# Perceiver block on one core: K and Q stored once in float32, brought back by heads, and split there

## The chip, the cores and the metric

The kernel runs on one core of one Trainium2 chip. Its time is the device time of one execution in microseconds (us). Engines: TensorE (PE) multiplies; VectorE (DVE), ScalarE (ACT) and GpSimd (POOL) work elementwise; SyncE (SP) only issues transfers (DMAs), as GpSimd does too. The engines run in parallel, each in its own order, and wait for each other through semaphores. A transfer is carried by up to 16 DMA engines.

## The reference

A perceiver block on 256 tokens of width 2048:

```
x = x + softmax(layernorm(x) @ ctx.T) @ ctx            # ctx: 25088 x 2048
h = layernorm(x);  q, k, v = h @ Wq + bq, h @ Wk + bk, h @ Wv + bv    # (token, d, head): 64 x 32, 64 x 8, 64 x 8
k, v = repeat(k, 4 heads), repeat(v, 4 heads)
scores[s, d, e] = sum over heads h of q[s, d, h] * k[s, e, h] / 8     # within one token: 64 x 64
x = x + (softmax(scores) @ v).reshape(2048)
h = layernorm(x);  x = x + h @ W_base.T + b_base + routed experts (8 of rank 16, top 2) of h
```

The second attention is between the 64 channels of one token, summed over heads. As K is repeated over groups of 4 heads, the kernel adds up Wq in groups of 4 columns beforehand, so Q and K both are 256 tokens x 8 groups x 64 channels, and the scores of a token are one product of an 8 x 64 matrix by another.

## The kernel before, in words

**Stages.** 49 blocks of 512 context rows come first (scores, running softmax, weighted sum); they fill the span to about 2213 us and are not touched. Then the attention result is normalised, and K, Q and V are projected (n = 0, 1, 2) from the 16 chunks of the normed x. Products in float32 are made of three passes over two parts: a rounded "hi" part (ScalarE casts it) and the rest "lo" (VectorE or GpSimd subtract). The weights of each projection come in 4 pieces by SyncE (`load_w_rows`, L518), get their hi part in `next_w_piece` (L839) on ScalarE and their lo part in `lo_w_piece` (L1199) on VectorE, and signal `nat_ready[j]`. Then follows the product of the normed x with w_base, in 64 chunks of 512 output columns (`base_chunk`, L1584), w = 0 to 63: GpSimd loads a chunk of 256 KB from wt_dram to one of four buffers `tr` (`load_base`, L659; it waits for the split of the chunk four before), ScalarE makes hi (`hi_base`, L865), VectorE lo (`lo_base`, L1223; each fourth is GpSimd's), TensorE multiplies. Hi waits too for the chunk four before to be used.

**K and Q by heads.** TensorE wants, for each token m, the 8 rows of K and of Q by groups on its partitions (`k_t`, `q_t`, [P, token, 64], bfloat16), in several bfloat16 parts: `K_PARTS` and `Q_PARTS` (L1748) say which of three parts lies in which of six sets of 8 partitions, for each half of the tokens. A float32 value is the sum of three bfloat16 parts: part 0 is a cast, part 1 a cast of the rest, part 2 the rest of the rest. They are made from PSUM in the layout token by (group, channel): `first_parts` (L854, ScalarE), `rests` (L1208, VectorE), `second_parts` (L860, ScalarE), `third_parts` (L1218, VectorE). SyncE stores the three parts in `qk_dram` with `store_qk` (L556): per tile of 128 tokens 3072 runs of 128 B. `heads_back` (L562) then waits until both tiles are stored and loads them back with 12 DMAs, each of 8 partitions by 16 KB.

**Order around it.** SyncE: the V weights, store of K (L569), the rows of lora_a (L572, in runs of 128 B), return of K (L574), store of Q (L575), return of Q (L578), b_base (L580). ScalarE (L883 to L898): first and second parts of K between the weight pieces, hi of w = 0 to 3, the V weight pieces, first and second parts of Q, copy of V, then hi of w = 4 and up (L915), with the groups of A, the gate and V's transposed groups (`v_group`, L900) put in after fixed chunks: those of `A_AFTER`, `GATE_AFTER`, `V_AFTER` (L1752 to L1756), each behind the hi of the chunk four further on. VectorE (L1238 to L1253) has the same order. TensorE: projection (L1564), `base_chunk` 0 to 15 with those groups (L1619); after w = 14 it waits for the returns of K and Q (L1643) and makes the scores of the first 8 of 128 pairs of tokens (`pair_scores`, L1597). After w = 15 each step has scores, transposes and three chunks.

Of the kernel before, what the change touches and what calls it, by code (L numbers as in the profile page):

```python
# [5 lines left out]
F32 = mybir.dt.float32  # L6
U32 = mybir.dt.uint32
ALU = mybir.AluOpType
# [4 lines left out]
BF16 = mybir.dt.bfloat16  # L13

P = 128
# [13 lines left out]
def perceiver_block(nc, x, ctx, wq, bq, wk, bk, wv, bv, w_base, b_base, w_gate, lora_a, lora_b, out):  # L29
# [11 lines left out]
    _, TOK, DIM = x.shape  # L41
    KEYS = ctx.shape[1]
    DH, HEADS = bq.shape
    KVH = bk.shape[1]
    REP = HEADS // KVH
    EXPERTS, RANK, _ = lora_a.shape
    OUTF = w_base.shape[0]
    TT = TOK // P
# [3 lines left out]
    NB = KEYS // KB  # L52
    PIECES = 4
    QKC = DH * KVH
# [57 lines left out]
    with ExitStack() as stack:  # L112
        def sem(name):
            return stack.enter_context(nc.semaphore(name))
# [10 lines left out]
        def put(at, name, shape, dt=F32):  # L125
            return nc.alloc_sbuf_tensor_at(name, shape, dt, offset=at)
# [7 lines left out]
        KIB = 1024  # L134
# [5 lines left out]
        at_probs = room(22 * KIB)  # L140
# [37 lines left out]
        w_rows = (put(at_quart + 24 * KIB, "w_rows0", [P, KT, BANK]), put(at_probs + 12 * KIB, "w_rows1", [P, KT, BANK]),  # L178
                  put(at_raw, "w_rows2", [P, KT, BANK]), put(at_raw + 8 * KIB, "w_rows3", [P, KT, BANK]))
        a_nat = put(at_quart + 24 * KIB, "a_nat", [P, DIM])  # L180
        k_nat = put(at_probs, "k_nat", [P, TT, 3, QKC], BF16)
        q_nat = put(at_quart, "q_nat", [P, TT, 3, QKC], BF16)
        qk_rest = put(at_quart + 6 * KIB, "qk_rest", [P, TT, QKC])
        a_sum = put(at_quart + 10 * KIB, "a_sum", [P, QKC])
# [80 lines left out]
        warm = late("warm", [P, 4])  # L265

        ps = stack.enter_context(nc.psum_tensor("ps", [P, 8, BANK], F32))
        qk_dram = nc.dram_tensor("qk_dram", (2, 3, KVH, TOK, DH), BF16)
        wq_dram = nc.dram_tensor("wq_dram", (DIM, QKC), F32)
        wt_dram = nc.dram_tensor("wt_dram", (DC, P, OUTF), F32)  # L270
        wp_dram = nc.dram_tensor("wp_dram", (PC, P, OUTF), F32)
# [18 lines left out]
        nat_ready = [sem(f"nat_ready{j}") for j in range(PIECES)]  # L290
# [25 lines left out]
        pool_split = sem("pool_split")  # L316
        w_used = sem("w_used")
        qkv_done = sem("qkv_done")
        qk_part1 = sem("qk_part1")
        qk_rested = sem("qk_rested")  # L320
        qk_part2 = sem("qk_part2")
# [98 lines left out]
        def _(sp):  # L420
# [14 lines left out]
            def load_in_chunks(to, src, a, done):  # L435

                sp.dma_start(to.rearrange("p (c a i) -> p a c i", a=QR, i=SQ)[:, a],
                             src[:, a * QF:(a + 1) * QF].rearrange("p (c i) -> p c i", i=SQ)).then_inc(done, 16)
# [112 lines left out]
            for n, rows in ((1, wq_rows), (2, wv_rows)):  # L551
                for j in range(PIECES):
                    sp.wait_ge(nat_ready[j], NB + n)
                    load_w_rows(j, rows)

            def store_qk(n, w, of):  # L556
                for t in range(TT):
                    sp.wait_ge(qk_split, TT * n + t + 1)
                    sp.dma_start(qk_dram[w, :, :, t * P:(t + 1) * P].rearrange("s g m d -> m (s g) d"),  # L559
                                 of[:, t].rearrange("p s (g d) -> p (s g) d", d=DH)).then_inc(qk_stored, 16)  # L560

            def heads_back(w, to, parts):  # L562
                sp.wait_ge(qk_stored, TT * (2 - w) * 16)
                for k, part in enumerate(parts):
                    for t in range(TT):
                        at = P // TT * t + KVH * k
                        sp.dma_start(to[at:at + KVH], qk_dram[w, part, :, t * P:(t + 1) * P]).then_inc(qk_back, 16)

            store_qk(0, 1, k_nat)  # L569
            sp.wait_ge(nat_ready[0], NB + 3)  # L570
            for a in range(QR):
                load_in_chunks(a_nat[:], lora_a.rearrange("e r d -> (e r) d"), a, a_loaded)  # L572
            sp.wait_ge(nat_ready[1], NB + 3)
            heads_back(1, k_t, K_PARTS)  # L574
            store_qk(1, 0, q_nat)  # L575
            for j in range(2, PIECES):
                sp.wait_ge(nat_ready[j], NB + 3)
# [155 lines left out]
        def _(act):  # L733
# [105 lines left out]
            def next_w_piece(n, j):  # L839
                if j < PIECES - 1:  # L840
                    w_piece(n, j, w_used, (PIECES - 1) * (n - 1) + j + 1)
                else:
                    w_piece(n, j, qkv_done, TT * n)
# [7 lines left out]
            deviation(1, 1)  # L851
            hi_x_tile(G_X1, 1)

            def first_parts(n, to):  # L854
                for t in range(TT):
                    act.wait_ge(qkv_done, n * TT + t + 1)
                    act.copy(to[:, t, 0].rearrange("p (g d) -> p g d", g=KVH),
                             ps[:, QKV_BANKS[n] + t, :].rearrange("p (d g) -> p g d", g=KVH)).then_inc(qk_part1, 1)

            def second_parts(n, to):  # L860
                for t in range(TT):
                    act.wait_ge(qk_rested, n * TT + t + 1)
                    act.copy(to[:, t, 1], qk_rest[:, t]).then_inc(qk_part2, 1)
# [18 lines left out]

            for j in range(PIECES - 1):  # L883
                next_w_piece(1, j)
            first_parts(0, k_nat)
            next_w_piece(1, PIECES - 1)
            second_parts(0, k_nat)
            for w in range(RING_CH):
                hi_base(w)
            for j in range(PIECES - 1):  # L890
                next_w_piece(2, j)
            next_w_piece(2, PIECES - 1)
            first_parts(1, q_nat)
            second_parts(1, q_nat)
            act.wait_ge(qkv_done, 3 * TT)
            src = ps[:, QKV_BANKS[2], :].rearrange("p (d g) -> p g d", g=KVH)
# [96 lines left out]
        def _(dve):  # L993
# [205 lines left out]
            def lo_w_piece(n, j):  # L1199
                dve.wait_ge(nat_hi_ready, (NB + n) * PIECES + j + 1)  # L1200
                dve.tensor_tensor(nat_lo[:, j], w_rows[j][:], nat_hi[:, j].bitcast(F32), ALU.subtract).then_inc(nat_ready[j], 1)  # L1201
# [3 lines left out]
            normalise(1, acc, x_nat)  # L1205
            lo_x_tile(G_X1, 1)

            def rests(n, of):  # L1208
                for t in range(TT):
                    dve.wait_ge(qk_part1, TT * n + t + 1)  # L1210
                    if n > 0:
                        dve.wait_ge(qk_split, TT * (n - 1) + t + 1)
                    dve.tensor_tensor(qk_rest[:, t].rearrange("p (g d) -> p g d", g=KVH),
                                      ps[:, QKV_BANKS[n] + t, :].rearrange("p (d g) -> p g d", g=KVH),
                                      of[:, t, 0].rearrange("p (g d) -> p g d", g=KVH),
                                      ALU.subtract).then_inc(qk_rested, 1)

            def third_parts(n, of):  # L1218
                for t in range(TT):
                    dve.wait_ge(qk_part2, TT * n + t + 1)  # L1220
                    dve.tensor_tensor(of[:, t, 2], qk_rest[:, t], of[:, t, 1], ALU.subtract).then_inc(qk_split, 1)
# [13 lines left out]
                dve.tensor_scalar(base_x[:, 1, ob * KB:(ob + 1) * KB], ps[:, 1, :], ln_b[:, 1:2], None,  # L1235
                                  ALU.mult).then_inc(base_kept[1], 1)

            for j in range(PIECES - 1):  # L1238
                lo_w_piece(1, j)
            rests(0, k_nat)  # L1240
            lo_w_piece(1, PIECES - 1)
            third_parts(0, k_nat)
            for w in range(RING_CH):
                if not by_pool(w):
                    lo_base(w)
            for j in range(PIECES):
                lo_w_piece(2, j)
            rests(1, q_nat)
            third_parts(1, q_nat)
            dve.wait_ge(qkv_done, 3 * TT)  # L1250
            src = ps[:, QKV_BANKS[2] + 1, :].rearrange("p (d g) -> p g d", g=KVH)
# [179 lines left out]
        def _(pe):  # L1431
# [132 lines left out]
            for n in (1, 2):  # L1564
                if n == 1:
                    pe.wait_ge(acc_updated, 8 * NB + 2)
                if n == 2:
                    pe.wait_ge(qk_rested, TT)
                for t in range(TT):
                    projection_bias(n, t)  # L1570
                for c in range(DC):
                    if c % 4 == 0:
                        pe.wait_ge(nat_ready[c // 4], NB + n + 1)
                    for t in range(TT):
                        projection(n, c, t)
# [43 lines left out]
            for w in range(PRE_W):  # L1619
                base_chunk(w)  # L1620
                if w in A_AFTER:
                    if 0 in A_AFTER[w]:
                        pe.wait_ge(a_loaded, 16 * QR)
                        pe.wait_ge(qk_rested, 2 * TT)
                    for g in A_AFTER[w]:
                        group(G_A + g, MID_BANK + (G_A + g) % 2, [chunk_cols(a_nat, 4 * g + a) for a in range(4)])
                if w == GATE_AFTER:
                    pe.wait_ge(gate_loaded, 16 * QR)
                    gate_group(G_GATE, side_rows, DC)
                if w == SUM_AFTER:  # L1630
                    pe.wait_ge(a_summed, 2 * (2 + PC))
                    group(G_SUM, MID_BANK + G_SUM % 2, [chunk_cols(a_sum, a) for a in range(PC)])
                if w == GSUM_AFTER:
                    gate_group(G_GSUM, gate_sum, PC)
                if w in V_AFTER:
                    if 0 in V_AFTER[w]:
                        for t in range(TT):
                            pe.wait_ge(v_copied[t], 2)
                    for k in V_AFTER[w]:
                        t, half = k // 2, k % 2  # L1640
                        plain_group(H_V + k, [v_dup[:, t, 4 * half + a].rearrange("p r e -> p (r e)") for a in range(4)])
                if w == PRE_W - 2:
                    pe.wait_ge(qk_back, 16 * TT * (len(Q_PARTS) + len(K_PARTS)))  # L1643
                    pe.wait_ge(lo_drained, G_GSUM + 1)
                    pair_scores(0)
# [136 lines left out]
```

## Time and profile before

| | us |
|---|---|
| median of 3 runs | 2508.55 (2503.86 to 2513.61) |
| profiled execution, its own time | 2506.24 |
| its span, first to last instruction | 2504.5 |
| TensorE busy | 2453.2 (98%) |
| VectorE, GpSimd, ScalarE busy | 1948.7, 1420.5, 1093.8 |
| mean granted clock of TensorE | 0.994 |

Busy time is time in which an instruction runs. The chain of waits follows the work back from the last instruction, at each step to what released it. Times in rows count from the start of the span. In a timeline row, the bracket at the end is the idle time of that engine just before and what ended it.

### The profile page before, as it was taken

To read this page: it belongs to the slowest core of one execution; us is meant where nothing else is said; L and a number is where in the kernel's file an instruction comes from. 1 tells how busy PE (TensorE), PEld (TensorE's weight loads), DVE (VectorE), ACT (ScalarE), POOL (GpSimd) and SP (SyncE) were. 2 spreads that over 40 slices of the span, in tenths; PEclk is the share of its full clock that TensorE was granted. 3 is DMA by queue.
4 is the path that set the end of the run, shared out by engine and by line. 5 is a ranking of instruction groups with operands and counts; after the bars stand their busy time and mean duration, and the time that the engine had idled before them with its cause. 6 is when DMAs were issued, how large, how long until landed. Compare 5 with 4: busy or idle time off the path is not lost.

```text
span 2504.5 us, 36094 instructions
## 1 busy us (share of the span) xinstructions
PE 2453.2 (98%) x11446; PEld 2009.8 (80%) x11446; DVE 1948.7 (78%) x2702; ACT 1093.8 (44%) x1576; POOL 1420.5 (57%) x1056
## 2 busy tenths in 40 slices
PE   6999999999999999999999999999999999999899
PEld 4788888888888888888888888888888888877677
DVE  7878888888888888888788887888878878674356
ACT  4444444444444444444444444444444444333443
POOL 4466666666666555565566565565555655652441
PEclk9999999999999999999999999999999999999899
DMA  9887878888788988889888988888888898778633
GB/s 239 212 229 203 229 210 220 224 206 229 206 229 217 224 206 219 222 211 218 212 219 204 230 212 204 219 217 219 211 219 216 205 222 217 199 169 155 153 122 101
DMA packets 421112, 518.22 MB, mean 207 GB/s; under 512 B 54407, under 2 KB 296071, under 8 KB 418441
## 3 DMA queue, kind: packets, MB, share of 16 engines
q1 hardware_dynamic: 411080, 475.66, 77.9%
q0 software_dynamic: 9984, 41.95, 5.0%
q8 instruction: 28, 0.46, 0.1%
q14 instruction: 20, 0.16, 0.0%
HBM read 488.71 MB, written 28.84 MB: 207 GB/s over the span
## 4 chain that ended last, share of the span: by engine, by line
PE 92%; DVE 3%; DMA 2%; SPq 1%; ACT 1%; issue 0%; POOL 0%; ACTq 0%; POOLq 0%
PE ps L1435 30%; PE ps L1437 30%; PE ps L1436 29%; PE ps L1444 2%; DMA tr<-wt_dram 2%; DVE ch_lo L1061 1%; SPq L429 1%; DMA raw<-in_ctx_dram 1%; SPq L559 0%; DVE tr L1057 0%; PE ps L1656 0%; DVE nat_lo L1201 0%; PE ps L1729 0%; PE ps L1602 0%; PE ps L1463 0%
## 5 line engine op out<-in xcount | busy, mean ns | idle before, releaser
L608 POOL TENSOR_TENSOR nat_lo<-raw,nat_hi 128x512 fp32r<-128x512 f32 x784 | 1170.9, 1523 | 874.0 <-ACT nat_hi L767 841.2
L1061 DVE TENSOR_TENSOR ch_lo<-tr,ch_hi 128x512 fp32r<-128x512 f32 x784 | 849.0, 1083 | 369.2 <-ACT ch_hi L756 369.2
L756 ACT CAST ch_hi<-tr 128x512 fp32r<-128x512 f32 x784 | 477.2, 621 | 807.6 <-PE ps L1437 799.4
L1435 PE MATMUL ps<-ch_hi,xt_hi 128*128 128x512 f32 x1696 | 680.1, 401 | 19.0 <-DVE ch_lo L1061 7.9
L1437 PE MATMUL ps<-ch_hi,xt_lo 128*128 128x512 f32 x1696 | 665.0, 392 | 0.0
L1436 PE MATMUL ps<-ch_lo,xt_hi 128*128 128x512 f32 x1696 | 664.1, 392 | 0.0
L1435 PE MATMUL ps<-nat_hi,pt_hi 128*128 128x512 f32 x1568 | 611.7, 390 | 2.1 <-DVE pt_lo L1010 2.1
L1437 PE MATMUL ps<-nat_hi,pt_lo 128*128 128x512 f32 x1568 | 610.3, 389 | 0.0
L1436 PE MATMUL ps<-nat_lo,pt_hi 128*128 128x512 f32 x1568 | 610.1, 389 | 0.0
L1057 DVE STREAM_TRANSPOSE tr<-quart 128x512 f32<-128x512 f32 x784 | 547.1, 698 | 0.0
L767 ACT CAST nat_hi<-raw 128x2048 fp32r<-128x2048 f32 x196 | 374.5, 1911 | 207.3 <-PE ps L1437 194.5
L1435 PEld LDWEIGHTS ps<-ch_hi,xt_hi 128*128 128x128 f32 x1696 | 320.4, 189 | 88.2 <-DVE ch_lo L1061 9.5
L1437 PEld LDWEIGHTS ps<-ch_hi,xt_lo 128*128 128x128 f32 x1696 | 320.1, 189 | 69.0
L1436 PEld LDWEIGHTS ps<-ch_lo,xt_hi 128*128 128x128 f32 x1696 | 321.0, 189 | 62.0
L1435 PEld LDWEIGHTS ps<-nat_hi,pt_hi 128*128 128x128 f32 x1568 | 294.3, 188 | 67.1 <-issue 3.4
L1437 PEld LDWEIGHTS ps<-nat_hi,pt_lo 128*128 128x128 f32 x1568 | 294.3, 188 | 61.4
L1436 PEld LDWEIGHTS ps<-nat_lo,pt_hi 128*128 128x128 f32 x1568 | 294.3, 188 | 60.8
L1099 DVE SCALAR_TENSOR_TENSOR acc<-acc,alpha,ps 128x512 f32<-128x512 f32 x248 | 177.8, 717 | 26.5 <-PE ps L1437 25.6
L740 ACT CAST pt_hi<-ps 128x512 fp32r<-128x512 f32 x98 | 57.2, 584 | 120.8 <-PE ps L1444 120.8
L1108 DVE SCALAR_TENSOR_TENSOR acc<-acc,alpha,ps 128x512 f32<-128x512 f32 x144 | 101.2, 703 | 4.9 <-PE ps L1437 4.9
L1226 DVE TENSOR_TENSOR ch_lo<-tr,ch_hi 128x512 fp32r<-128x512 f32 x56 | 40.9, 737 | 77.3 <-ACT ch_hi L872 76.9
L773 ACT ACTIVATE probs<-ps,neg_max 128x512 f32<-128x512 f32 x98 | 67.1, 685 | 77.4 <-DVE neg_max L1081 77.4
(199 smaller groups left out, 1312.7 us busy)
## 6 DMA issues: line engine op xcount, KB each, us to landing
quart<-in_ctx_dram SPq DMA_DIRECT2D x392, 512.0 KB, 8.3
raw<-in_ctx_dram SPq DMA_DIRECT2D x196, 1024.0 KB, 8.3
wq_in<-in_L_attn_Wq_dram POOLq DMA_DIRECT2D x16, 1024.0 KB, 6.3
win<-in_L_ffn_W_base_dram SPq DMA_DIRECT2D x64, 256.0 KB, 6.8
tr<-wt_dram POOLq DMA_DIRECT2D x64, 256.0 KB, 3.2
wt_dram<-stage SPq DMA_DIRECT2D x32, 256.0 KB, 5.6
wt_dram<-stage_b SPq DMA_DIRECT2D x32, 256.0 KB, 10.3
wq_dram<-wq_out POOLq DMA_DIRECT2D x16, 256.0 KB, 2.3
```

The source lines that it names most:

```text
L608: last = pool.tensor_tensor(nat_lo[:, j, t], raw[:, j % 2, t], nat_hi[:, j, t].bitcast(F32), ALU.subtract)
L740: act.copy(dst, src).then_inc(hi_drained, 1)
L756: act.copy(ch_hi[:, c % RING_CH, :], tr[:, c % RING_TR, :]).then_inc(chunk_hi, 1)
L767: act.copy(nat_hi[:, j], raw[:, j % 2]).then_inc(nat_hi_ready, 1)
L773: act.activation(probs[:, q, :], ps[:, SCORE_BANK + TT * new + q, :], ACT.Exp, bias=neg_max[:, new, q:q + 1], accum_out=row_sum[:, q:q + 1 ...
L1057: dve.transpose(tr[:, c % RING_TR, :].rearrange("p (r i) -> p r i", i=SQ), src).then_inc(chunk_transposed, 1)
L1061: dve.tensor_tensor(ch_lo[:, c % RING_CH, :], tr[:, c % RING_TR, :], ch_hi[:, c % RING_CH, :].bitcast(F32), ALU.subtract).then_inc(chunk_s ...
L1099: dve.scalar_tensor_tensor(piece, piece, alpha[:, 1 - turn.parity, q:q + 1], ps[:, out_bank(v, turn.over), :], ALU.mult, ALU.add).then_inc ...
L1108: dve.scalar_tensor_tensor(piece, piece, alpha[:, turn.parity, q:q + 1], ps[:, out_bank(v, False), :], ALU.mult, ALU.add).then_inc(acc_upd ...
L1435: pe.matmul(out_, a_hi, b_hi, start=start, stop=False)
L1436: pe.matmul(out_, a_hi, b_lo, start=False, stop=False)
L1437: return pe.matmul(out_, a_lo, b_hi, start=False, stop=stop)
```

## The change

K and Q are copied from PSUM once, in float32, to `k_full` and `q_full` (ScalarE, `full_copy`), stored to a new `full_dram` in runs of 256 B (`store_full`), and come back with each partition holding 8 tokens of one group, a run of 2 KB (`full_by_heads`). The three parts are made there, as before but from SBUF, and `store_qk` stores them in runs of 1 KB. `heads_back` loads the same bytes in the same DMAs of 8 partitions by 16 KB, from a `qk_dram` in which each tile's part is contiguous. The orders: SyncE stores and brings back K before it loads lora_a, stores K's parts behind that, then stores Q, returns K by heads, brings Q's rows back, stores Q's parts. ScalarE and VectorE make K's parts between the second and third V weight piece, and Q's before V's copy, where they were. TensorE waits for `qk_copied` where it waited for `qk_rested`.

```diff
-        k_nat = put(at_probs, "k_nat", [P, TT, 3, QKC], BF16)
+        k_full = put(at_probs, "k_full", [P, TT, QKC])
+        k_nat = put(at_probs + 4 * KIB, "k_nat", [P, TT, 3, QKC], BF16)
+        q_full = put(at_probs + 16 * KIB, "q_full", [P, TT, QKC])
...
-        qk_dram = nc.dram_tensor("qk_dram", (2, 3, KVH, TOK, DH), BF16)
+        qk_dram = nc.dram_tensor("qk_dram", (2, 3, TT, KVH, P, DH), BF16)
+        full_dram = nc.dram_tensor("full_dram", (2, TT, KVH, P, DH), F32)
...
+            def store_full(n, of):
+                for t in range(TT):
+                    sp.wait_ge(qk_copied, TT * n + t + 1)
+                    sp.dma_start(full_dram[n, t].rearrange("g m d -> m g d"),
+                                 of[:, t].rearrange("p (g d) -> p g d", d=DH)).then_inc(full_stored[n][t], 16)
+
+            def full_by_heads(n, to):
+                for t in range(TT):
+                    sp.wait_ge(full_stored[n][t], 16)
+                    sp.dma_start(to[:, t], full_dram[n, t].rearrange("g (a b) d -> (g a) (b d)", a=P // KVH)
+                                 ).then_inc(full_back[n][t], 16)
+
             def store_qk(n, w, of):
                 for t in range(TT):
                     sp.wait_ge(qk_split, TT * n + t + 1)
-                    sp.dma_start(qk_dram[w, :, :, t * P:(t + 1) * P].rearrange("s g m d -> m (s g) d"),
-                                 of[:, t].rearrange("p s (g d) -> p (s g) d", d=DH)).then_inc(qk_stored, 16)
+                    sp.dma_start(qk_dram[w, :, t].rearrange("s g (a b) d -> (g a) s (b d)", a=P // KVH),
+                                 of[:, t]).then_inc(qk_stored, 16)
...
-                        sp.dma_start(to[at:at + KVH], qk_dram[w, part, :, t * P:(t + 1) * P]).then_inc(qk_back, 16)
-
-            store_qk(0, 1, k_nat)
+                        sp.dma_start(to[at:at + KVH], qk_dram[w, part, t]).then_inc(qk_back, 16)
+
+            store_full(0, k_full)
+            full_by_heads(0, k_full)
             sp.wait_ge(nat_ready[0], NB + 3)
             for a in range(QR):
                 load_in_chunks(a_nat[:], lora_a.rearrange("e r d -> (e r) d"), a, a_loaded)
+            store_qk(0, 1, k_nat)
+            store_full(1, q_full)
             sp.wait_ge(nat_ready[1], NB + 3)
             heads_back(1, k_t, K_PARTS)
+            full_by_heads(1, q_full)
             store_qk(1, 0, q_nat)
...
-            def first_parts(n, to):
+            def full_copy(n, to):
                 for t in range(TT):
                     act.wait_ge(qkv_done, n * TT + t + 1)
-                    act.copy(to[:, t, 0].rearrange("p (g d) -> p g d", g=KVH),
-                             ps[:, QKV_BANKS[n] + t, :].rearrange("p (d g) -> p g d", g=KVH)).then_inc(qk_part1, 1)
+                    act.copy(to[:, t].rearrange("p (g d) -> p g d", g=KVH),
+                             ps[:, QKV_BANKS[n] + t, :].rearrange("p (d g) -> p g d", g=KVH)).then_inc(qk_copied, 1)
+
+            def first_parts(n, of, to):
+                for t in range(TT):
+                    act.wait_ge(full_back[n][t], 16)
+                    act.copy(to[:, t, 0], of[:, t]).then_inc(qk_part1, 1)
...
-            first_parts(0, k_nat)
+            full_copy(0, k_full)
             next_w_piece(1, PIECES - 1)
-            second_parts(0, k_nat)
             for w in range(RING_CH):
                 hi_base(w)
-            for j in range(PIECES - 1):
+            for j in range(2):
                 next_w_piece(2, j)
+            first_parts(0, k_full, k_nat)
+            second_parts(0, k_nat)
+            next_w_piece(2, 2)
+            act.wait_ge(nat_ready[1], NB + 3)
+            full_copy(1, q_full)
             next_w_piece(2, PIECES - 1)
-            first_parts(1, q_nat)
+            first_parts(1, q_full, q_nat)
             second_parts(1, q_nat)
...
-                    dve.tensor_tensor(qk_rest[:, t].rearrange("p (g d) -> p g d", g=KVH),
...
+                    dve.tensor_tensor(qk_rest[:, t], full[:, t], of[:, t, 0], ALU.subtract).then_inc(qk_rested, 1)
...
-            for j in range(PIECES - 1):
+            for j in range(PIECES):
                 lo_w_piece(1, j)
-            rests(0, k_nat)
-            lo_w_piece(1, PIECES - 1)
-            third_parts(0, k_nat)
             for w in range(RING_CH):
                 if not by_pool(w):
                     lo_base(w)
-            for j in range(PIECES):
+            for j in range(2):
                 lo_w_piece(2, j)
-            rests(1, q_nat)
+            rests(0, k_full, k_nat)
+            third_parts(0, k_nat)
+            for j in range(2, PIECES):
+                lo_w_piece(2, j)
+            rests(1, q_full, q_nat)
             third_parts(1, q_nat)
...
                 if n == 2:
-                    pe.wait_ge(qk_rested, TT)
+                    pe.wait_ge(qk_copied, TT)
...
-                        pe.wait_ge(qk_rested, 2 * TT)
+                        pe.wait_ge(qk_copied, 2 * TT)
```

## Rows read from the trace of the kernel before

**Rows 1.** The chain that ended last, share of the span by engine.

```profile
PE 92%; DVE 3%; DMA 2%; SPq 1%; ACT 1%; issue 0%; POOL 0%; ACTq 0%; POOLq 0%
```

**Rows 2.** Stretches: us; PE, PEld, DVE, ACT, POOL busy (x); PEclk, DMA share, GB/s.

```profile
2282.00:2306.00 24.00, 24.00 (x102) 18.83 (x102) 6.08 (x5) 4.08 (x5) 8.07 (x11) 1.00 0.80 113
...
2312.00:2332.00 20.00, 18.67 (x106) 14.71 (x106) 8.24 (x15) 9.99 (x19) 7.97 (x12) 1.00 0.91 179
...
2340.00:2356.00 16.00, 12.43 (x56) 8.82 (x57) 6.29 (x10) 8.74 (x13) 7.16 (x10) 0.52 0.50 163
```

**Rows 3.** Timeline of TensorE: start, us, operation, idle before and its end.

```profile
2340.34 0.79 PE L1435 MATMUL ps<-ch_hi,xt_hi 128*128 128x512 f32 x1 [7.27 <-DVE ch_lo L1226]
...
2345.39 0.87 PE L1602 MATMUL ps<-k_t,q_t 48*64 48x64 bf16 x16 [2.13 <-DMA q_t<-qk_dram]
```

**Rows 4.** Timeline of SyncE's issues, 2263 to 2325 us.

```profile
2263.87 10.39 SPq L559 DMA_DIRECT2D qk_dram<-k_nat  x2
2274.31 8.01 SPq L437 DMA_DIRECT2D a_nat<-in_L_ffn_A_dram  x4
2282.43 6.12 SPq L567 DMA_DIRECT2D k_t<-qk_dram  x12
2288.93 25.34 SPq L559 DMA_DIRECT2D qk_dram<-q_nat  x2
2319.64 4.47 SPq L567 DMA_DIRECT2D q_t<-qk_dram  x12
```

**Rows 5.** DMA view of 2272.5:2278, 2278.5:2285.5, 2286:2290 and 2326:2330, in this order.

```profile
DMA packets 6199, 0.85 MB, mean 155 GB/s; under 512 B 6173, under 2 KB 6173, under 8 KB 6198
...
DMA packets 7676, 0.98 MB, mean 141 GB/s; under 512 B 7675, under 2 KB 7675, under 8 KB 7675
...
q1 hardware_dynamic: 82, 0.27, 51.7%
...
q1 hardware_dynamic: 68, 0.56, 96.4%
```

**Rows 6.** Landing: K store; Q store; tiles issued 2290:2296; tiles issued after 2354.

```profile
DMA to landing us min/median/max: 12.5/13.7/14.9
...
DMA to landing us min/median/max: 27.2/28.2/29.1
...
DMA to landing us min/median/max: 17.3/18.2/19.2
...
DMA to landing us min/median/max: 2.8/2.9/4.9
```

**Rows 7.** Timeline of ScalarE: hi of w = 4, 13, V's copies, w = 14, 15, 16.

```profile
2310.66 1.16 ACT L872 CAST ch_hi<-tr 128x512 fp32r<-128x512 f32 x2 [3.43 <-DMA tr<-wt_dram]
...
2326.51 0.62 ACT L872 CAST ch_hi<-tr 128x512 fp32r<-128x512 f32 x1 [2.08 <-DMA tr<-wt_dram]
2327.04 2.57 ACT L907 COPY v_t<-ps 64x256 f32<-64x256 f32 x4
2338.94 0.62 ACT L872 CAST ch_hi<-tr 128x512 fp32r<-128x512 f32 x1 [9.34 <-DMA tr<-wt_dram]
2342.61 0.62 ACT L872 CAST ch_hi<-tr 128x512 fp32r<-128x512 f32 x1 [3.05 <-DMA tr<-wt_dram]
...
2345.85 0.62 ACT L872 CAST ch_hi<-tr 128x512 fp32r<-128x512 f32 x1
```

**Rows 8.** Timeline of GpSimd: loads of w = 13, 14 and 16 issued.

```profile
2319.09 0.54 POOL L671 DMA_DIRECT2D tr<-wt_dram  x1 [0.20 <-issue]
2321.78 0.54 POOL L671 DMA_DIRECT2D tr<-wt_dram  x1 [2.15 <-DVE ch_lo L1226]
...
2325.46 0.54 POOL L671 DMA_DIRECT2D tr<-wt_dram  x1 [0.74 <-DVE ch_lo L1226]
```

**Rows 9.** K's first and third parts: duration ns min/median/max, starts, shapes.

```profile
L857 ACT CAST k_nat<-ps x2: 572/578/585, 2255.9 to 2256.8; 128x512 bf16<-128x512 f32 x2
...
L1221 DVE TENSOR_TENSOR k_nat<-qk_rest,k_nat x2: 684/686/687, 2261.7 to 2262.3; 128x512 bf16<-128x512 f32 x2
```

More of the change, by code:

```diff
@@ L318, in perceiver_block @@
         qkv_done = sem("qkv_done")
+        qk_copied = sem("qk_copied")
+        full_stored = [[sem(f"full_stored{n}_{t}") for t in range(TT)] for n in range(2)]
+        full_back = [[sem(f"full_back{n}_{t}") for t in range(TT)] for n in range(2)]
         qk_part1 = sem("qk_part1")
@@ L1206, in _, with rests @@
             lo_x_tile(G_X1, 1)
-            def rests(n, of):
+            def rests(n, full, of):
                 for t in range(TT):
@@ L1212, in rests @@
                         dve.wait_ge(qk_split, TT * (n - 1) + t + 1)
-                    dve.tensor_tensor(qk_rest[:, t].rearrange("p (g d) -> p g d", g=KVH),
-                                      ps[:, QKV_BANKS[n] + t, :].rearrange("p (d g) -> p g d", g=KVH),
-                                      of[:, t, 0].rearrange("p (g d) -> p g d", g=KVH),
-                                      ALU.subtract).then_inc(qk_rested, 1)
+                    dve.tensor_tensor(qk_rest[:, t], full[:, t], of[:, t, 0], ALU.subtract).then_inc(qk_rested, 1)
             def third_parts(n, of):
```

## The prediction

> **What bounds the kernel now.** I read the chain of waits first: TensorE holds 92% of it [rows 1], and the 49 blocks of context, some 2200 us, are full. The change touches none of that. It touches the stretch from 2255 to 2355 us, where K, Q and V are projected and the first 16 chunks of w_base (I call them w = 0 to 15, and their 256 KB loads from wt_dram "tiles") are multiplied. So the second view is busy time by stretch [rows 2]: TensorE is full until 2312, then has 18.67 of the 20 us to 2332 and 12.43 of the 16 from 2340, these at a granted clock of 0.52, about its lower level of 1.2 GHz. The TensorE timeline [rows 3] names the holes: 7.27 us before w = 14, which waited for its low part and behind it for its tile (ScalarE sat 9.34 us on the transfer, [rows 7]), and 2.13 us for q_t.
>
> Behind both stands one thing, read from SyncE's row [rows 4] beside the DMA view [rows 5]. The return of K by heads (12 DMAs, each 8 partitions by 16 KB) is issued at 2282.43, the one of Q at 2319.64. While the K return runs alone (2286 to 2290) the hardware queue moves 0.27 MB and fills only 51.7% of the 16 engines: half the engines carry it, at 67 GB/s. All 12, 1.57 MB, take 23.4 us at that rate. The store of Q is issued at 2288.93 behind it and lands 27 to 29 us later [rows 6], although SyncE's second half of that issue was merely stuck on the queue. Q's own return then takes from 2319.64 to the first scores at 2345.39, 25.75 us. Tiles that are loaded beside such a return land after 17.3 to 19.2 us, and after 2.8 to 4.9 once it is over [rows 6].
>
> **The change, part by part.** Call S the time at which the return of Q is first issued; now S = 2319.64.
>
> *K out.* The K copies read PSUM as the first parts did (0.58 us each, [rows 9]) and cost nothing new. The store is now 2048 pieces of 256 B instead of 6144 of 128 B. The latter ran from about 2272.5, when the V weights were through, to 2278: 0.85 MB in 5.5 us, 155 GB/s [rows 5]. Half a megabyte takes 1.8 us if the cost goes by pieces (2048 of 6199 in 5.5 us) and 3.4 us if it goes by bytes; I take 2.5 and 1.2 for landing, so 2276.2. It landed at 2279.2 (2264.3 plus 14.9).
>
> *K back in rows.* New: two loads of 256 KB, 128 rows of 2 KB each. Nearest row: a tile of the same size and row length, 2.8 to 4.9 us; with a busy queue 17. I take 3, so 2279.2. SyncE waits there, and behind it stand only the lora_a loads: they were issued from 2274.31 over 8.01 us, and start now at 2276.5.
>
> *K's parts.* Two casts, two subtractions, two casts, two subtractions, staggered over the two tiles, 0.58 and 0.69 us each: four links and one extra, 2.7 us, so 2281.9. This wait is new on ScalarE and VectorE. Behind it on ScalarE is the third V weight piece, which starts at 2281 rather than 2276.9 and whose low part is done at 2285.2. TensorE is full from 2282 to 2306 with V's 16 chunks [rows 2], 1.4 us each from 2284, and wants this piece at the ninth, 2295. Cover 10 us: cost nothing. If the K rows came after 2289 it would cost TensorE one for one.
>
> *K's store.* 0.79 MB in pieces of 1 KB, issued behind lora_a. lora_a's small pieces drained until 2285.5 [rows 5], and shift to about 2286. At 200 GB/s the store needs 3.7 us and lands at 2290.9, between 2289 and 2293 (by 155 GB/s). The Q copy's store (0.5 MB) is ahead of the return in the queue and fits into that landing. The K return moves from 2282.43, with data from 2285.5, to data from 2292: about 7 us later, ended at 2316.3 and not 2309.5.
>
> *Q back in rows.* In SyncE's order `full_by_heads(1, ...)` comes after `heads_back(1, ...)`. Its rows use all engines, hence also the half that is busy until 2316.3. So it lands at 2319.8 at best: 0.5 MB is 2.4 us, 1.1 for landing. From below: were it not held it would land near 2300; from above, if it fares as a tile beside a return, 2323.
>
> *Q's parts and store.* 3.0 us for the chain, until 2322.8; the store, 0.79 MB, lands 5.2 us later (its second half took as much after SyncE came free at 2314.3). S = 2328.0, 8.4 us later than now. What is removed, the 25.34 us in which SyncE was held at L559, buys nothing: nobody but this same return stood behind it, and the K return ahead of it stays.
>
> *Who waits behind Q's parts.* On both engines the copies of V and then all splits of w = 4 and up stand behind them. Now hi of w = 4 ran at 2310.66 [rows 7]; it will be 2323.1, after two V copies of 0.6 us each. TensorE has w = 0 to 3, ends them at 2312.3 and then idles until A's third group at 2326.3: 14 us. By itself this is hidden, since TensorE now waits at w = 14 until 2340.3 anyhow. But the tiles fall behind: there are four buffers, and the load of w + 4 is issued after the split of w. Now the load of w = 13 is issued 0.55 us before S, w = 14 at S + 2.1, w = 16 at S + 5.8 [rows 8], and they are cast at S + 6.9, S + 19.3 and S + 26.2, w = 15 at S + 23.0 [rows 7]: a tile issued after S comes near the end of the Q return. In the new order the loads of w = 11, 12 and 13 are issued at about S + 1.4, S + 3.3 and S + 5.8. So tile 13 is cast between S + 23.0 (as w = 15 now) and S + 26.2 (as w = 16). And two of V's transposed groups, which TensorE needs after w = 11, are copied by ScalarE behind the cast of w = 13: 2.57 us more [rows 7]. TensorE then does w = 12, 13, 14 and the first scores; q_t is there by then.
>
> **The sum.** TensorE took up w = 14 at 2340.34. It will take up w = 12 at S + 23.0 or S + 26.2, plus 0.6 for the cast, 2.6 for the V copies and 0.6 for the transposes: 2354.8 or 2358.0, which is 14.5 or 17.7 later. Two chunks more than now are left, 2.7 us at the full clock. The 2.13 us for q_t go. The 15 us at the low clock after the wait I leave as they are. That is +15.1 or +18.3; I take +16. On the profiled execution's own 2506.24 us (span 2504.5) this makes 2522. The median shown is 2508.55, 2.3 above that execution, so the median of the new kernel is 2524.5.
>
> **A rule weighed.** A tile loaded beside a head return needs 17.3 to 19.2 us, against 2.8 to 4.9 alone [rows 6], and from 2326 to 2330 the hardware queue alone fills 96.4% [rows 5]. The Trainium skill, "DMA: Bandwidth & Descriptors", section "Queues, rings and completion order", says that an engine takes turns between queues, a packet from each. By it a tile would be held for little more than one 16 KB packet a turn and come in some 5 us. The trace disagrees. What the rule would give is rival 1.
>
> **Rivals.**
> 1. *Only q_t counts.* If the tiles issued after S come in 5 to 7 us (4.9 is the most without a return [rows 6], the last one before S was cast after 7.4), TensorE is through w = 14 by 2350 and waits for q_t at S + 25.75 = 2353.8: +8.4, against nothing else. 2515 to 2518. Against it: four tiles of before, all late. For it: TensorE's 14 us hole spreads the loads otherwise.
> 2. *The small pieces were the trouble: faster.* If the return of Q's rows is not held by the K return (the half of the engines that is free does its work, or the K return runs faster from a packed source), the rows are back at 2300 and the store of Q lands near 2309. S is 10 us earlier, w = 14 finds its tile, the first scores come at 2334.4 in place of 2345.39, and the low clock with its some 4 us more goes too: -15, 2493.5; if only the store still waits for the K return, S is 2318 and it is -1. It decides on whether Q's rows land before about 2309. The Trainium skill, same page, section "Specifications", holds transfers under 512 B to be slow, which speaks for it. Against: the first half of Q's store was held 27 us by the same return, in the same queue.
> 3. *V starves as well.* If K's rows come at 2290 or later, as when the 256 B pieces or their landing are slow behind the V weights, every us beyond 2289 stops TensorE in V, and S moves too: +25, 2533.
> 4. *The change does nothing.* Q's chain costs what the blocked issue cost (10 us between the end of the K return and S, both ways), and K's shift is absorbed: 2505 to 2512.
>
> **How the numbers follow.** Forecast 0.55 (its own range 2514 to 2534), rival 1 0.20, rival 2 0.07, rival 3 0.08, rival 4 0.10. The range 2506 to 2536 leaves out most of rival 2 and the tail of 3. A measurement here tells about 0.5%, 12.5 us, from no change: the border is 2521. Slower takes 0.8 of the forecast, rival 3 and a quarter of rival 1, together 0.57; faster half of rival 2 and a little, 0.05; the rest 0.38.
>
> **What would show it.** The first return DMA of Q (S) at about 2328 and the one of K at 2291; the first K cast at 2278; the load of Q's rows landing about 2320, some 22 us after its issue; TensorE idle from 2312 to 2326 for A's group, released by the split behind Q's parts, and again after w = 11; tiles issued after S landing after 17 us. Wrong it would be if Q's rows landed before 2312, if S were under 2322, or if the tiles in the Q return came in 6 us.

## The result: 0.65% slower, and the profile after

The changed kernel takes 2523.24 us (median of 8 runs, 2517.92 to 2531.31), the kernel before 2508.02 (8 runs, 2501.57 to 2513.61): ratio 1.0065, 95% interval 1.0048 to 1.0083. The forecast was 2524.5. In the experiments below, one execution of e8 (6369 us) and one of the kernel before beside e5 to e8 (3524 us) are far off all the others and are in no ratio. The profiled execution, 2517.92 us with a span of 2516.4, is the fastest of its eight: it is 11.7 us over the profiled one of before, while the medians are 15.2 apart.

SyncE's timeline of the changed kernel, to be read beside [rows 4]:

```profile
2275.01 1.49 SPq L571 DMA_DIRECT2D k_full<-full_dram  x2
2276.54 6.12 SPq L443 DMA_DIRECT2D a_nat<-in_L_ffn_A_dram  x4
2282.71 2.22 SPq L577 DMA_DIRECT2D qk_dram<-k_nat  x2
...
2288.55 4.08 SPq L585 DMA_DIRECT2D k_t<-qk_dram  x12
2292.67 0.83 SPq L571 DMA_DIRECT2D q_full<-full_dram  x2
2322.51 0.97 SPq L577 DMA_DIRECT2D qk_dram<-q_nat  x2
2326.29 4.99 SPq L585 DMA_DIRECT2D q_t<-qk_dram  x12
```

Nothing holds SyncE for 25 us any more, and it buys nothing: the return of K (12 DMAs) is issued 6.1 us later, the return of Q (S) 6.65 us later. Between them, the load of Q's rows is issued at 2292.67 and not used before 2319.77. The waits of the changed kernel (engine, line, waited for: us in total, times, longest), 2255 to 2372 us:

```profile
ACT q_nat L885 <- DMA q_full<-full_dram: 34.0, 1, 34.0
...
ACT ch_hi L899 <- DMA tr<-wt_dram: 16.5, 5, 6.0
...
PE ps L1473 <- DVE ag_lo L1041: 13.3, 1, 13.3
```

ScalarE stands 34 us for those rows, with everything for w = 4 and up behind it. Its timeline, beside [rows 7]:

```profile
2319.77 1.14 ACT L885 CAST q_nat<-q_full 128x512 bf16<-128x512 f32 x2 [33.95 <-DMA q_full<-full_dram]
...
2323.22 1.15 ACT L899 CAST ch_hi<-tr 128x512 fp32r<-128x512 f32 x2
...
2351.13 0.62 ACT L899 CAST ch_hi<-tr 128x512 fp32r<-128x512 f32 x1 [1.28 <-DMA tr<-wt_dram]
```

The last row is hi of w = 13, at S + 24.8. TensorE's timeline, beside [rows 3], shows four holes: a long one before A's third group (released by a split that stands behind Q's parts), two for the low parts of w = 10 and 11, whose tiles come late, and one after w = 11 (for V's copies behind hi of w = 13). There is no wait for q_t.

```profile
2326.15 1.97 PE L1473 MATMUL ps<-ident,a_nat 128*128 128x128 f32 x8 [13.34 <-DVE ag_lo L1041]
...
2343.21 0.50 PE L1464 MATMUL ps<-ch_hi,xt_hi 128*128 128x512 f32 x1 [2.31 <-DVE ch_lo L1254]
...
2347.26 0.80 PE L1464 MATMUL ps<-ch_hi,xt_hi 128*128 128x512 f32 x1 [2.22 <-POOL ch_lo L698]
...
2352.98 1.11 PE L1492 MATMUL ps<-ident,v_dup 128*128 128x128 f32 x4 [2.79 <-ACT v_t L938]
...
2360.84 0.59 PE L1631 MATMUL ps<-k_t,q_t 48*64 48x64 bf16 x16
...
2364.58 0.47 PE L1464 MATMUL ps<-ch_hi,xt_hi 128*128 128x512 f32 x1 [1.05 <-ACT base_x L907]
```

The first scores come 15.45 us later than before, w = 16 13.5 us later, the end of the span 11.9. The difference is where the lower level of the clock falls, in the stretches (columns as in [rows 2]):

```profile
2312.00:2332.00 20.00, 6.67 (x24) 5.18 (x22) 8.76 (x14) 8.17 (x15) 3.44 (x5) 0.66 0.51 137
2332.00:2340.00 8.00, 8.00 (x51) 6.41 (x51) 1.00 (x3) 0.79 (x2) 1.08 (x2) 1.00 0.97 171
2340.00:2356.00 16.00, 8.50 (x31) 5.84 (x30) 3.56 (x6) 7.20 (x13) 3.54 (x6) 0.64 0.58 173
2356.00:2372.00 16.00, 14.95 (x90) 11.70 (x89) 7.39 (x11) 10.40 (x17) 9.31 (x13) 0.93 0.41 133
```

Before, the clock was at 0.52 from 2340 to 2356, with w = 14, the first scores and w = 15 and 16 in it. After, there are two low stretches, 0.51 from 2317 to 2331 us and 0.50 from 2344.5 to 2358. TensorE waits in about half of them and otherwise does w = 4, 11 and 12 and some groups (0.63 us a product of a chunk in place of 0.39), all ahead of the first scores, which run at the upper level (0.59 us for 16 small products and not 0.87). The work at the lower level has not shrunk, it has moved: TensorE is busy for 11.9 us of it before and 13.2 after.

### The profile page after: what moved, and what is told of

Read it like the earlier page. It is cut to its first block, busy times and chain, and to the rows that moved or that the text cites. A ratio compares the mean times of both kernels' runs of the same rounds, so it can differ in the third digit from the quotient of the medians.

```text
span 2516.4 us, 36107 instructions
## 1 busy us (share of the span) xinstructions
PE 2453.2 (97%) x11446; PEld 2010.0 (80%) x11446; DVE 1949.2 (77%) x2702; ACT 1094.3 (43%) x1580; POOL 1422.6 (57%) x1056
## 4 chain that ended last, share of the span: by engine, by line
PE 92%; DMA 3%; DVE 3%; SPq 1%; ACT 1%; issue 0%; POOL 0%; ACTq 0%; POOLq 0%
PE ps L1464 30%; PE ps L1466 29%; PE ps L1465 29%; PE ps L1473 2%; DMA q_full<-full_dram 1%; DMA tr<-wt_dram 1%; DMA raw<-in_ctx_dram 1%; DVE ch_lo L1092 1%; SPq L435 1%; DMA full_dram<-k_full 0%; PE ps L1492 0%; DVE tr L1088 0%; PE ps L1685 0%; PE ps L1631 0%; PE ps L1758 0%
```

## The experiments

S is always the first issue of Q's return. Ratios are against the kernel before, run beside each on the same chip; medians of different experiments can come from different chips.

**e1, rows of Q first.**

```diff
-            heads_back(1, k_t, K_PARTS)
             full_by_heads(1, q_full)
+            heads_back(1, k_t, K_PARTS)
```

> The changed kernel, but SyncE brings Q's rows back (2 loads of 256 KB) before the return of K by heads instead of behind it. Theory: Q's rows are late only because they stand behind the K return on the half of the engines that it holds. Then they land near 2293 us instead of 2319.7, Q's parts are done by 2297 on idle engines, hi of w = 4 runs at about 2307 instead of 2323, and the 13.3 us hole of TensorE before A's third group goes. The K return starts 1 to 2 us later and the store of Q still waits behind it, S about 2320 to 2322. Time: the changed kernel minus 12 to 16 us, i.e. 2508 to 2512, level with the kernel before. Rival (the extra trips through DRAM cost by themselves): hole stays, 2520 to 2525.

Measured: 2516.11 us, ratio 1.0032 (1.0016 to 1.0049): half of the loss is left, and the time is above the expected 2508 to 2512. Q's rows are cast at 2291.1 and 2293.5: that part held to the us. SyncE and then TensorE of e1:

```profile
2288.45 1.35 SPq L571 DMA_DIRECT2D q_full<-full_dram  x2
2289.84 4.04 SPq L585 DMA_DIRECT2D k_t<-qk_dram  x12
...
2321.00 4.09 SPq L585 DMA_DIRECT2D q_t<-qk_dram  x12
```

```profile
2317.79 1.97 PE L1473 MATMUL ps<-ident,a_nat 128*128 128x128 f32 x8 [6.92 <-DVE ag_lo L1041]
...
2338.23 0.80 PE L1464 MATMUL ps<-ch_hi,xt_hi 128*128 128x512 f32 x1 [4.35 <-POOL ch_lo L698]
...
2351.51 1.12 PE L1492 MATMUL ps<-ident,v_dup 128*128 128x128 f32 x4 [10.35 <-ACT v_t L938]
```

A hole of 6.92 us stays that I had not seen coming: the tiles of w = 4 to 7, issued at 2292.3, land beside K's return, now 7 us later than before:

```profile
DMA to landing us min/median/max: 18.1/23.7/24.7
```

In the changed kernel this was true too (20.0 to 24.9 us) and lay hidden behind Q's parts. And hi of w = 13 comes at 2349.7 although S is 5 us earlier: S + 28.7. The tiles asked for after S land one after the other, at 2336.2, 2343.9, 2349.6 (w = 13) and 2353.6 us, and the last piece of the return at 2352.1. The profiled execution lies at the median of e1, that of the changed kernel below its own: the two are only 1.5 us apart, and TensorE's holes add up to about the same (21.8 and 20.8 us). Where the 7 us between the medians went, these two traces do not show.

**e2, only K by the new way.** Q's parts from PSUM, store in runs of 128 B, as before.

```diff
-            store_full(1, q_full)
...
-            full_by_heads(1, q_full)
-            store_qk(1, 0, q_nat)
+            store_old(1, q_nat)
```

> Only K takes the new way; Q is split from PSUM, stored in runs of 128 B and returned as in the kernel before. Theory: the K return moves from 2282.4 to about 2288, S by as much to about 2325, no hole at 2312 because nothing of Q stands before the splits of w = 4 and up; two more tiles are asked for before S, so only q_t counts: kernel before plus 4 to 7 us, 2512 to 2515. Rival (the K side is hidden, all of the loss is Q's): equal to before, 2508.

Measured: 2517.95 us, ratio 1.0029 (1.0012 to 1.0047): within what was expected by the ratio (+7 us), above it by the median. S is 2321.37 and not 2325, with K's return at 2288.21. SyncE and TensorE of e2:

```profile
2288.21 4.02 SPq L586 DMA_DIRECT2D k_t<-qk_dram  x12
2292.28 23.79 SPq L591 DMA_DIRECT2D old_dram<-q_nat  x2
2321.37 4.74 SPq L599 DMA_DIRECT2D q_t<-old_dram  x12
```

```profile
2315.90 1.26 PE L1499 MATMUL ps<-ident,a_nat 128*128 128x128 f32 x8 [2.45 <-DVE ag_lo L1057]
...
2335.05 1.08 PE L1518 MATMUL ps<-ident,v_dup 128*128 128x128 f32 x4 [3.73 <-ACT v_t L954]
...
2345.75 0.88 PE L1657 MATMUL ps<-k_t,q_t 48*64 48x64 bf16 x16 [3.59 <-DMA q_t<-old_dram]
```

The store of Q took up most of K's shift: S is 1.7 us later than before, not 5.8. The profiled execution (2506.49 us) is the fastest of ten, and its first scores are 0.4 us later than before: it does not show the loss. That K's half costs something rests on the ratio alone, whose interval leaves out 1; by that the rival (equal to before) falls, and where the time goes is not shown.

**e3, only Q by the new way.**

```diff
-            store_full(0, k_full)
-            full_by_heads(0, k_full)
+            store_old(0, k_nat)
...
-            heads_back(1, k_t, K_PARTS)
+            heads_old(1, k_t, K_PARTS)
             full_by_heads(1, q_full)
```

> Only Q takes the new way; K is as in the kernel before. Theory: the K return starts at about 2284 and ends at 2311, Q's rows land at about 2314, hole of TensorE before A's third group about 8 us instead of 13.3, S about 2321. Kernel before plus 4 to 9 us, 2512 to 2517. If the rise is not additive with that of K only, one of the two is covered by the other. Rival (Q's rows are held by their own wait for the store and not by the K return): rows before 2300, no hole, 2508.

Measured: 2521.59 us, ratio 1.0051 (1.0034 to 1.0067), above the expected 2512 to 2517. TensorE of e3:

```profile
2324.97 1.97 PE L1500 MATMUL ps<-ident,a_nat 128*128 128x128 f32 x8 [12.76 <-DVE ag_lo L1057]
...
2345.48 0.79 PE L1491 MATMUL ps<-ch_hi,xt_hi 128*128 128x512 f32 x1 [6.54 <-DVE ch_lo L1280]
...
2356.19 1.12 PE L1519 MATMUL ps<-ident,v_dup 128*128 128x128 f32 x4 [4.18 <-ACT v_t L954]
```

The first hole is nearly that of the changed kernel although K's return starts 2 us earlier, at 2286.56: its last piece comes at 2316.0 all the same (2316.9 in the changed kernel). For the tile of w = 10 TensorE waits nearly three times as long as in the changed kernel. Q's half carries most of the loss (0.51%), K's 0.29%; together 0.80%, and 0.65% with both, inside the intervals.

**e4, Q's parts after w = 7.** No transfer is moved, only ScalarE's and VectorE's order.

```diff
-            first_parts(1, q_full, q_nat)
-            second_parts(1, q_nat)
...
+                if w == 7:
+                    first_parts(1, q_full, q_nat)
+                    second_parts(1, q_nat)
```

(and `rests`, `third_parts` on VectorE likewise)

> The changed kernel, but ScalarE and VectorE make Q's parts after the splits of w = 4 to 7 instead of before V's copies; no transfer is changed. Theory: the rows still land at 2319.7 and S stays at 2326, but the hole of 13.3 us at 2312 shrinks to some 5 us after w = 7, and four more tiles are loaded or asked for before S. Then q_t at S + 25.7 = 2352 is the end of the stage (the first scores were 16 us later than before, now 7): the changed kernel minus 6 to 9 us, 2514 to 2517. Rival (the tiles do not matter, only q_t does): no difference to the changed kernel.

Measured: 2513.45 us, ratio 1.0012 (0.9995 to 1.0029). TensorE of e4:

```profile
2316.31 1.97 PE L1475 MATMUL ps<-ident,a_nat 128*128 128x128 f32 x8 [5.75 <-DVE ag_lo L1042]
...
2340.37 0.80 PE L1466 MATMUL ps<-ch_hi,xt_hi 128*128 128x512 f32 x1 [3.59 <-DVE ch_lo L1255]
...
2350.12 0.87 PE L1633 MATMUL ps<-k_t,q_t 48*64 48x64 bf16 x16 [6.82 <-DMA q_t<-qk_dram]
```

S is 2325.45, almost that of the changed kernel, and still some 10 us come back by the medians (0.53 of the 0.65% by the ratios). So by these what stood behind Q's parts is the larger part of the loss. Between the two profiled executions it is 4.6 us of 11.7, as much as the holes shrink (16.2 us in place of 20.8). The rest is not clear of noise, as the interval holds 1; in the trace it is the wait for q_t and a hole for the tile of w = 14. The hole of 5.75 us is, as in e1, for the tiles of w = 4 to 7.

**e5, returns of 48 partitions.** The six sets lie in DRAM one after the other, some stored twice.

```diff
-                for k, part in enumerate(parts):
-                    for t in range(TT):
-                        at = P // TT * t + KVH * k
-                        sp.dma_start(to[at:at + KVH], qk_dram[w, part, t]).then_inc(qk_back, 16)
+                for t in range(TT):
+                    sp.dma_start(to[P // TT * t:P // TT * t + 6 * KVH],
+                                 qk_dram[w, t].rearrange("s g m d -> (s g) m d")).then_inc(qk_back, 16)
...
-Q_PARTS = (0, 0, 1, 1, 0, 2)
-K_PARTS = (0, 1, 0, 1, 2, 0)
+Q_PARTS = (0, 1, 2, 1, 0, 0)
+K_PARTS = (0, 1, 0, 0, 1, 2)
+SLOTS = (((0, 0, 3), (3, 1, 1), (4, 0, 1), (5, 0, 1)), ((0, 0, 2), (2, 0, 1), (3, 0, 3)))
```

(`store_qk` issues one DMA per entry of SLOTS: slot, first part, number of parts.)

> The changed kernel, with qk_dram holding all six sets of parts (some stored twice: 1.57 MB instead of 0.79) and each return by heads as 2 DMAs of 48 partitions by 16 KB instead of 12 of 8 partitions. Theory: the returns are slow (1.57 MB in 23 us) because only half the engines carry 8 partitions, and everything late stands behind them. Then each return takes about 12 us. K's is over near 2305, Q's rows land near 2307 instead of 2319.7, the hole of TensorE at 2312 shrinks from 13.3 to 2 or 3 us, S is 2315 to 2318, q_t is there by 2331, and the tiles come in under 10 us. Time: 2494 to 2502, 22 to 28 us under the changed kernel. Rival (the return is bound by what one 16 KB partition row takes or by DRAM, not by the number of engines): no change of its 23 us and 3 us more for the larger store, 2523 to 2528.

Measured: 2504.42 us, ratio 0.998 (0.9963 to 0.9997), a little above the expected 2494 to 2502; 19 us under the changed kernel's median, with the same bytes returned and more stored. One DMA of the return (KB, us to landing), from 2290 to 2294 us, and the hole that is left on TensorE:

```profile
k_t<-qk_dram SPq DMA_DIRECT2D x1, 768.0 KB, 12.6
```

```profile
2336.29 1.11 PE L1492 MATMUL ps<-ident,v_dup 128*128 128x128 f32 x4 [8.57 <-ACT v_t L938]
```

Q's rows are cast from 2304.6, the hole at 2312 is 0.55 us, S is 2317.7. The number of partitions set the pace of the return, and not DRAM or the number of DMAs: a row of 16 KB took an engine 1.9 us before and 1.7 here (medians of K's 96 rows), but on the average 7 rows were under way at a time before and 15 here. What I missed is that tiles still wait beside a return of 12 us: those issued from 2318 to 2323 land after 13.5 to 15.3 us.

**e6, the same returns in the kernel before.**

```diff
+                    for slot, part, many in SLOTS[w]:
+                        sp.dma_start(qk_dram[w, t, slot:slot + many].rearrange("s g m d -> m (s g) d"),
+                                     of[:, t, part:part + many].rearrange("p s (g d) -> p (s g) d", d=DH)).then_inc(qk_stored, 16)
```

> The kernel before, with the same six sets and returns of 48 partitions; the stores stay in runs of 128 B and are now 12288 runs each. Theory: returns of 12 us each outweigh the 6 us more for each store; S about 2316, scores on time: 2498 to 2504. If the small runs were the trouble of the kernel before, doubling them should cost more than it gives: 2508 or above.

Measured: 2499.36 us, ratio 0.9953 (0.9937 to 0.9969), with 12288 runs of 128 B in each store, twice as many as before. The DMA view of e6 from 2290 to 2292 us, in K's return, answers to the third row of [rows 5]; TensorE's one hole is below it.

```profile
q1 hardware_dynamic: 19, 0.31, 94.1%
```

```profile
2330.53 1.12 PE L1463 MATMUL ps<-ident,v_dup 128*128 128x128 f32 x4 [4.79 <-ACT v_t L907]
```

0.31 MB in 2 us is 155 GB/s over all engines, against 67 GB/s over half of them. Over the whole of K's return it is less: 1.57 MB from 2289.7 to 2300.5 us, 146 GB/s, and 64 before (2285.6 to 2310.1). The small runs were then not the main trouble of the kernel before: with twice as many of them it is faster, and e7 below, which stores none of 128 B, is no faster than e6. What they cost by themselves no run isolates.

**e7, e5 with Q's rows first.**

> As e5 and, as in e1, Q's rows come back before the return of K. Theory: Q's parts are made near 2297, no hole but what the tiles of w = 4 to 7 cost beside a return of 12 us (they land by 2306), S near 2312, q_t by 2326, so TensorE never waits for q_t and the clock stays at its upper level: 2492 to 2498. If the order no longer matters once the return is wide, equal to e5 within 2 us.

Measured: 2502.68 us, ratio 0.9959 (0.9941 to 0.9977). No hole at 2312, S 2317.07, and a hole of 8.24 us after w = 11. Above the expected 2492 to 2498: w = 12's and 13's tiles are caught beside Q's return as in e5.

**e8, e1 with the tiles of w = 4 to 7 issued before GpSimd's sums.**

```diff
             pool.wait_ge(a_loaded, 16 * QR)
-            sums(a_nat, a_sum, slice(0, P), 2 + PC)
             lo_base(3)
             for w in range(RING_TR, 2 * RING_TR):
                 load_base(w)
+            sums(a_nat, a_sum, slice(0, P), 2 + PC)
```

> As e1 (returns of 8 partitions), and GpSimd issues the loads of w = 4 to 7 before its sums over lora_a, some 5 us earlier, at 2287 and so ahead of the return of K. In e1 hi of w = 4 waited for its tile until 2310.4 and of w = 5 until 2315.8, which left a hole of 6.9 us: these four tiles were caught beside the return of K. Theory: ahead of it they land by 2293, hi of w = 4 runs at 2307, the hole goes, the tiles of w = 12 and 13 are asked for before S: 2508 to 2511, level with the kernel before. Rival (the tiles are slow for another reason): as e1, 2516.

Measured: 2513.08 us, ratio 1.0005 (0.9986 to 1.0024), against the 2508 to 2511 expected. Hi of w = 4 runs at 2305.87, as V ends, and the holes for tiles are gone but for 2.48 us. TensorE of e8 then waits for q_t alone, and long, in a profiled execution (2516.35 us) that is above the median:

```profile
2321.35 0.41 PE L1642 MATMUL ps<-ident,gate_sum 8*128 8x8 f32 x4 [2.48 <-DVE ag_lo L1040]
...
2351.45 0.87 PE L1630 MATMUL ps<-k_t,q_t 48*64 48x64 bf16 x16 [16.54 <-DMA q_t<-qk_dram]
```

**e9, e10, e11: what holds the tiles beside Q's return.** In e9 the load of b_base waits for the landed return (on e6); e11 has besides V's groups two chunks later; e10 is both on e7.

```diff
+            sp.wait_ge(qk_back, 16 * TT * 2)
             sp.wait_ge(qkv_done, 3 * TT)
             sp.dma_start(b_base_all[:], b_base.unsqueeze(0).broadcast_to([P, OUTF])).then_inc(bias_loaded, 16)
...
-V_AFTER = {9: (0, 1), 11: (2, 3)}
+V_AFTER = {11: (0, 1), 13: (2, 3)}
```

> e6 with the load of b_base (1 MB, the same 8 KB to 128 partitions) issued after the return of Q has landed instead of right behind its issue. In e6 TensorE still waited 4.8 us after w = 11 for V's copies, which stand behind hi of w = 13, whose tile was caught beside Q's return and b_base. Theory: that 1 MB is part of what holds the tiles; without it they come 3 to 5 us earlier and the wait falls to 0 to 2 us: 2495 to 2498, against 2499.4 for e6. Rival (the return of Q alone holds them): as e6.

> e7 (all new paths, rows of Q first, returns of 48 partitions), b_base late as in e9, and V's groups after w = 11 and 13 instead of 9 and 11, so that TensorE needs V's copies two chunks later. Theory: of the 8.2 us hole of e7 (V's copies behind the cast of w = 13) 3 to 5 us go with b_base and the rest mostly with the order, since w = 12 and 13 can run meanwhile: 2492 to 2497, against 2502.7 for e7. If only tiles count and not who stands behind the cast, the order gives nothing: 2498.

> e9 with V's groups after w = 11 and 13. Theory: what is left of the hole after w = 11 goes, 2493 to 2497; if TensorE waits for the tile of w = 14 or for q_t right after, equal to e9.

Measured: 2499.5 us, ratio 0.9971 (0.9959 to 0.9983); 2499.01, ratio 0.9966 (0.9948 to 0.9984); 2499.96, ratio 0.996 (0.9947 to 0.9973). None beats e6 by the ratio, and all three are above what was expected (2495 to 2498, 2492 to 2497, 2493 to 2497). The largest hole of each, in this order:

```profile
2332.68 1.11 PE L1464 MATMUL ps<-ident,v_dup 128*128 128x128 f32 x4 [5.09 <-ACT v_t L908]
```

```profile
2331.76 0.80 PE L1465 MATMUL ps<-ch_hi,xt_hi 128*128 128x512 f32 x1 [5.80 <-POOL ch_lo L699]
```

```profile
2334.08 0.80 PE L1436 MATMUL ps<-ch_hi,xt_hi 128*128 128x512 f32 x1 [4.72 <-DVE ch_lo L1227]
```

b_base was not what held them, and moving V's groups only moves the hole to the tile itself. The four tiles issued from 2316 to 2323 us land after 9.1 to 13.6 us in e9 and 12.6 to 13.5 in e6. Without b_base the later ones come somewhat sooner, but the first, asked for 0.6 us after S, lands at 2330.1 in e9, with the last piece of the return at 2329.0, and from 2319.5 us until then only the return and these tiles are in flight.

## Why the prediction was right, step by step

- *K out and back:* SyncE issued the K rows' loads at 2275.0 and 2275.9 (I had the landing of the stores at 2276.2), the K casts ran at 2277.8 and 2279.2 (2279.2 for the last). The V weight piece behind them was 4 us later than before, and V lost nothing, as costed.
- *K's store:* expected to land at 2290.9 and S of K at about 2291; it was 2288.48 for the landing and 2288.55 for S of K. I had taken 200 GB/s for runs of 1 KB (which makes 3.9 us of 0.79 MB, and not the 3.7 I wrote). The changed kernel's hardware queue from 2286 to 2288, and the landing of the K store:

```profile
q1 hardware_dynamic: 929, 0.75, 110.5%
...
DMA to landing us min/median/max: 4.0/4.4/4.8
```

- *Q's rows:* expected at 2319.8, cast at 2319.77. That the two agree so well is luck, as two errors cancel: the data of K's return started at 2289.7 and not at 2292, and it ran to 2316.9, 27.2 us where I had 24.3. Why it took longer no run isolates. That the rows were late because of that return is shown by e1 (issued ahead of it they land after 2.6 and 4.0 us, behind it after 27.1) and by e5.
- *Q's parts and store:* chain done at 2323.1 (2322.8). The store was issued at 2322.51 and landed in 2.6 to 3.1 us, not 5.2, so S was 2326.3 and not 2328.0, +6.65 and not +8.4: a term sized by the nearest row, a store of 128 B runs.
- *Who waits behind:* hi of w = 4 at 2323.22 (2323.1), TensorE idle 13.34 us (14). The tiles: w = 10, 11 and 12 were asked for at S + 1.3, S + 3.5 and S + 6.1, one chunk fewer than I had: S itself was 1.7 us earlier, while the split of w = 4 was on time, and TensorE came out of the hole at the lower clock level (0.66 in 2312 to 2332). They took 14.2 to 16.8 us. Still hi of w = 13 ran at S + 24.8, between my S + 23.0 and S + 26.2, although it was asked for at S + 10.4 and not S + 5.8. e1 says that this was not a rule but partly luck: there it was asked for at S + 4.5 and ran at S + 28.7. I had read before that a tile issued after S comes near the end of the return; w = 10 and 11 landed 7.5 and 4.0 us ahead of it (2349.2).
- *The sum:* my two bounds were +15.1 and +18.3, and I took +16; the first scores came 15.45 us later. The term that was mis-sized is the stretch at the low clock after the wait, which I had left as it was: it now lies ahead of the scores, and 3.5 us came back behind them. So the profiled execution, for which the sum was made, is +11.7 and not +16. The medians are +15.2, and that they come so near the forecast is in part luck: their extra is not explained by one trace, of the fastest of eight executions. The interval of the ratio, 12 to 21 us, holds the forecast; +11.7 lies just below it.

The rule that was weighed and would have given rival 1: the tiles issued after S and more than 3 us before the end of the return landed after 9.9 to 16.8 us here, after 11.5 to 25.4 in e1 and after 9.1 to 13.6 in e9, never in 5. The Trainium skill ("DMA: Bandwidth & Descriptors", section "Queues, rings and completion order") has an engine drain a whole packet of one queue, typically some 9 to 17 descriptors, before it switches to the next. That a turn is one row of 16 KB, from which the 5 us came, was my own assumption and not the page's: the trace speaks against those 5 us, and how long a turn is no run shows. The 96.4% read beside it [rows 5] are not the return's alone either: b_base, issued at 2324.16 in the same queue, is in that window, and no packet of GpSimd's queue is, with three tiles asked for. The same page's section "Why a DMA increments its semaphore by 16 and not by 1" picks the number of engines from the outermost size (8 partitions: 8 engines); this agrees with 51.7% and 94.1% of the engines' time for 8 and 48 partitions.

Rival 1's case appeared in e8 and e4: with the tiles out of the way the first scores wait for q_t until S + 28.8 and S + 24.7, and the time is 0 to 0.2% over before. Rival 2 asked for Q's rows before 2309; they landed at 2319.7. Rival 3 did not occur (K's rows were there at 2279.2), and rival 4, no change, is outside the interval of the ratio. What stays open is why a tile in GpSimd's queue is held so long beside a return in SyncE's: no run changed the size of the return's rows, or issued it from another queue.

## What to carry to other kernels

Before counting runs or bytes of a transfer, ask how many partitions its SBUF side has: here 8 partitions filled half the DMA engines, and with 48 in a transfer the kernel before became 0.47% faster although its small runs doubled, while the change that removed the small runs made it 0.65% slower. A transfer that was issued behind a long one in the same queue landed only with that one's end (27.1 us for Q's rows, 2.6 to 4.0 when issued ahead), so put what compute waits for first. And a wait put on an engine early costs what stands behind it in that engine's order: here four weight buffers fell behind, and by the medians (e4) that was worth more than the late q_t itself.

## What the hardware showed that I had not expected

Stores with runs of mostly 1 KB (677 of the 929 packets) moved 0.75 MB in 2 us (375 GB/s), and a store of 0.79 MB landed in 2.6 to 3.1 us, against 155 GB/s for runs of 128 B. The tiles of w = 4 to 7, issued beside K's return in the changed kernel, took 20.0 to 24.9 us each:

```profile
DMA to landing us min/median/max: 20.0/24.3/24.9
```
